# Loads of u and B reshaped from 36 rows three partitions apart to 64 rows two apart, with a staged part of zeros

## What is computed

```python
xc = silu(conv(normed @ in_proj_W) + conv_b)            # (8, 512, 256)
dt = clip(softplus(xc @ dt_W + dt_b), 0.001, 0.1)
Bp, Cp = xc @ B_W, xc @ C_W                             # (8, 512, 64)
def step(h, ins):                                       # 512 steps in sequence
    x_t, dt_t, B_t, C_t = ins
    h = exp(dt_t[..., None] * A) * h + dt_t[..., None] * B_t[:, None, :] * x_t[..., None]
    return h, einsum('ben,bn->be', h, C_t)
_, y = scan(step, h0, (xc, dt, Bp, Cp))
x = x + (y * silu(z)) @ out_proj_W ; x = x + feed_forward(x)
out = xn_input + block(xn) + binary_network(xn)
```

## Times and profile before

| | us |
|---|---|
| median of 3 runs | 1122.29 |
| lowest and highest run | 1107.89, 1122.53 |
| profiled execution, its own time | 1115.98 |
| its span, first to last instruction | 1114.2 |

### The profile page before, as it was taken

One profiled execution on the slowest core, in us unless ns is written; L12 is line 12 of the kernel. 1 busy time (PEld: TensorE's weight loads), 2 busy tenths in 40 slices (PEclk: granted clock), 3 DMA queues, 4 the chain that ended last, 5 costly groups with the idle time before them and its releaser, 6 DMA issues.

```text
span 1114.2 us, 27718 instructions
## 1 busy us (share of the span) xinstructions
PE 967.9 (87%) x8006; PEld 426.6 (38%) x8006; DVE 935.2 (84%) x2131; ACT 908.7 (82%) x1093; POOL 847.9 (76%) x1216
## 2 busy tenths in 40 slices
PE   5998883668999999998999887899998899999897
PEld 3555540113333343433333332334343334343436
DVE  5677663799989999997998887899998899999983
ACT  1666776789999999997988887899997899998980
POOL 6555513789888889887888786898887788988880
PEclk9999996789999999999999999899999899999999
DMA  4234358999999999997999999799999799999940
GB/s 139 81 136 180 136 200 298 345 327 355 351 343 334 345 355 350 345 344 268 356 341 332 319 328 318 271 351 352 353 349 333 280 366 343 339 356 340 335 148 10
DMA packets 76758, 327.39 MB, mean 294 GB/s; under 512 B 13472, under 2 KB 32800, under 8 KB 41504
## 3 DMA queue, kind: packets, MB, share of 16 engines
q1 hardware_dynamic: 76576, 325.30, 83.6%
HBM read 303.24 MB, written 22.02 MB: 292 GB/s over the span
## 4 chain that ended last, share of the span: by engine, by line
DVE 27%; PE 25%; POOL 19%; issue 16%; DMA 5%; ACT 5%; SPq 2%; DVEq 1%; POOLq 0%; ACTq 0%
POOL decayed L593 13%; DVE ps L1221 9%; PE ps L798 8%; DVE state L1232 7%; PE ps L743 5%; PE ps L897 5%; DMA decay<-dt_stage 4%; PE ps L883 3%; DVE h L1336 2%; ACT state L1030 2%; DVE h L1345 1%; DVE soft L1147 1%; POOL soft L543 1%; SPq L392 1%; POOL u_rest L553 1%
## 5 line engine op out<-in xcount | busy, mean ns | idle before, releaser
L593 POOL TENSOR_TENSOR decayed<-decay,state 128x256 f32<-128x256 f32 x1024 | 725.5, 733 | 169.1 <-DVE state L1232 125.4
L1010 ACT ACTIVATE decay<-decay,a_col 128x2048 f32<-128x2048 f32 x256 | 512.7, 2003 | 46.3 <-DMA decay<-dt_stage 36.5
L1232 DVE TENSOR_TENSOR state<-decayed,ps 128x256 f32<-128x256 f32 x1024 | 403.1, 417 | 55.4 <-POOL decayed L593 40.0
L1221 DVE TENSOR_TENSOR ps<-decay,ps 128x512 f32<-128x512 f32 x512 | 352.6, 689 | 40.5 <-ACT state L1030 17.2
L1030 ACT COPY state<-ps 128x512 f32<-128x512 f32 x512 | 288.9, 582 | 64.6 <-issue 43.2
L798 PE MATMUL ps<-state,c_cols 128*32 128x256 f32 x4096 | 338.2, 403 | 0.1
L743 PE MATMUL ps<-moving,b_rows 64*128 64x256 bf16 x1024 | 204.3, 281 | 100.5 <-DVE ps L1221 96.3
L750 PE MATMUL ps<-moving,b_rows 64*128 64x256 bf16 x1024 | 205.4, 282 | 12.0 <-DMA b_rows<-b_stage 12.0
L883 PE MATMUL ps<-h,w 128*128 128x256 f32 x512 | 175.8, 429 | 1.0 <-DVE h L1336 0.8
L743 PEld LDWEIGHTS ps<-moving,b_rows 64*128 64x128 bf16 x1024 | 58.4, 94 | 274.0 <-DVE ps L1221 172.3
L798 PEld LDWEIGHTS ps<-state,c_cols 128*32 128x32 f32 x4096 | 82.0, 109 | 113.4 <-issue 101.3
(11 more groups left out here) (124 smaller groups left out, 825.3 us busy)
## 6 DMA issues: line engine op xcount, KB each, us to landing
decay<-dt_stage SPq DMA_DIRECT2D x512, 512.0 KB, 6.6
moving<-u_stage SPq DMA_DIRECT2D x64, 288.0 KB
b_stage<-b_parts SPq DMA_DIRECT2D x24, 384.0 KB, 3.8
b_rows<-b_stage SPq DMA_DIRECT2D x64, 144.0 KB
dt_stage<-dt_tok SPq DMA_DIRECT2D x8, 512.0 KB, 3.1
u_stage<-u_parts SPq DMA_DIRECT2D x8, 512.0 KB, 2.8
x_tok<-in_L_attn_x_dram SPq DMA_DIRECT2D x4, 512.0 KB, 3.5
u_stage<-u_parts SPq DMA_DIRECT2D x8, 256.0 KB, 2.1
```

The costliest lines, as they stand in the source:

```text
L593: nc.gpsimd.tensor_tensor(decayed[:, p], decay[:, dec_slot(m, k), p, k % TS, :], state[:, (k - 1) % RING, p * E:(p + 1) * E], ALU.mult).th ...
L1010: nc.scalar.activation(pair, pair, ACT.Exp, scale=a_col[:, 2:3]).then_inc(decay_ready, 1)
L1221: nc.vector.tensor_tensor(ps[:, acc_bank(m, k), :].rearrange("p (q e) -> p q e", q=HQ), decay[:, dec_slot(m, k), HQ:Q, k % TS, :], ps[:, a ...
L1232: nc.vector.tensor_tensor(state[:, k % RING, p * E:(p + 1) * E], decayed[:, p], ps[:, SELFP + k % 2, p * E:(p + 1) * E], ALU.add).then_inc ...
```

## The change

`u_stage` and `b_stage` get a fourth part (NS = 4) along each dimension of parts, which holds zeros. It is written once, in the front, by 24 stores from a zeroed piece of `moving` (`store_pads`): for each of the 8 batches 256 KB to `u_stage`, and 512 KB and 384 KB to `b_stage`. `load_u` then moves 16 rows of 8 KB, each four times, and `load_b` 64 rows of 4 KB, both to the 64 partitions hq, hq + 2, hq + 4 and so on, which are the partitions of a dt transfer. All 128 rows of `moving` are now loaded, so that its two memsets go; a smaller one on POOL (2048 elements of a partition) makes the zeros for the stores.

```diff
-    ROWS = NP * NP * HALF
-    RSTEP = 3
-    RFIRST = HROW + RSTEP - 1 - RSTEP * (ROWS // 2)
+    NS = NP + 1
+    ROWS = NS * NS * HALF
+    assert HQ * ROWS == P
-    u_stage = nc.dram_tensor("u_stage", (HQ, HQ, 2, NP, T, E), BF16, kind="Internal").ap()
+    u_stage = nc.dram_tensor("u_stage", (HQ, HQ, 2, NS, T, E), BF16, kind="Internal").ap()
-    b_stage = nc.dram_tensor("b_stage", (HQ, HQ, 2, NP, NP, T, 2 * N), BF16, kind="Internal").ap()
+    b_stage = nc.dram_tensor("b_stage", (HQ, HQ, 2, NS, NS, T, 2 * N), BF16, kind="Internal").ap()
...
-            first = RFIRST - 2 + hq
-            return slice(first, first + RSTEP * (ROWS - 1) + 1, RSTEP)
+            return slice(hq, P, HQ)
...
-                         .unsqueeze(1).broadcast_to([HALF * NP, NP, TC * E])
+                         .unsqueeze(1).broadcast_to([HALF * NS, NS, TC * E])
...
+                def store_pads(n):
+                    q, bb = n // 2, n % 2
+                    u_rows, b_planes = u_stage[q % HQ, q // HQ, bb], b_stage[q % HQ, q // HQ, bb]
+                    zeros = moving[:, 1, 0:2 * NS].rearrange("p t e -> p (t e)")
+                    sp.dma_start(u_rows[NP].rearrange("(p j) e -> p (j e)", j=NJ),
+                                 zeros[:, 0:NJ * E]).then_inc(pads_stored, 16)
+                    sp.dma_start(b_planes[NP].rearrange("k (p j) n -> p k (j n)", j=NJ),
+                                 zeros[:, 0:NS * NJ * 2 * N].rearrange("p (k n) -> p k n", k=NS)).then_inc(pads_stored, 16)
+                    sp.dma_start(b_planes[0:NP, NP].rearrange("k (p j) n -> p k (j n)", j=NJ),
+                                 zeros[:, 0:NP * NJ * 2 * N].rearrange("p (k n) -> p k n", k=NP)).then_inc(pads_stored, 16)
...
+                sp.wait_ge(pad_zeroed, 1)
+                for n in range(B):
+                    store_pads(n)
...
                 sp.wait_ge(rows_zeroed, 2)
+                sp.wait_ge(pads_stored, 16 * PADS)
...
+                nc.gpsimd.memset(moving[:, 1, 0:2 * NS], 0.0).then_inc(pad_zeroed, 1)
...
-                    nc.gpsimd.memset(moving[:, 0], 0.0)
                     nc.gpsimd.memset(b_rows[:, 0], 0.0).then_inc(rows_zeroed, 1)
...
-                    nc.vector.memset(moving[:, 1], 0.0)
                     nc.vector.memset(b_rows[:, 1], 0.0).then_inc(rows_zeroed, 1)
```

More of the change, by code:

```diff
@@ L46, in mamba_and_binary_mlp_block @@
     HROW = P // 2
-    ROWS = NP * NP * HALF
-    RSTEP = 3
-    RFIRST = HROW + RSTEP - 1 - RSTEP * (ROWS // 2)
-    assert RFIRST > 0 and HROW + HQ - 1 + RSTEP * (ROWS // 2) <= P
+    NS = NP + 1
+    ROWS = NS * NS * HALF
+    assert HQ * ROWS == P
     QE = Q * E
@@ L118, in mamba_and_binary_mlp_block @@
         b_loaded = [sem("b_loaded0"), sem("b_loaded1")]
+        pad_zeroed = sem("pad_zeroed")
         rows_zeroed = sem("rows_zeroed")
+        pads_stored = sem("pads_stored")
         const_set = sem("const_set")
@@ L212, in mamba_and_binary_mlp_block @@
         STORES = 2 + NP
+        PADS = 3 * B
         def batches(eng, slot, filling=None):
```

## The result

| | median of the runs | profiled execution | its span |
|---|---|---|---|
| before | 1122.41 us | 1115.98 us | 1114.2 us |
| after | 1182.84 us (1179.76 to 1184.77) | 1184.77 us | 1183.0 us |

The account below looks back on a forecast made before the run. Engines were taken to set a floor of 27.05 us a chunk, with DMA binding now and then; 1116.0 - 17.3 + 2 - 1.5 - 1.5 gave 1097.7, say 1098 us. The forecast's own range was 1086 to 1106, the overall range 1086 to 1165.

Parts of the forecast that it names:

- The floor and the need: Scan: engines set 27.05 us a chunk (16 steps, 8 exps); after the change that needs 373 GB/s, up from 348.
- The sum: Whole kernel: 1116.0 us less 17.3, plus 2, less 1.5, less 1.5 gives 1097.7 us; chance 0.48.
- -1.5 for the front: Front: the `moving` memset on DVE goes, saving 1.5 us (0 to 2.1).
- +2 - 1.5 for the start: Scan's start: larger first u and B transfers cost 2 us; no longer slowing dt rows beside the second set saves 1.5.
- -17.3 for the rest: Scan outside the loop starts: stalls of the exps for dt go, saving 17.3 us (bounds 0 and 17.3).
- the 24 stores of zeros: Front: 11.8 us of SP's issuing and 9.4 MB of writes, covered by over 7 us, so costing 0.
- Bytes and marks: Chunk's transfers: 9.40 MB becomes 10.09 MB; u/B transfers go from 12 engines to 16, with 16 completion marks each.
- Why the mix is slow: Scan, u/B beside dt: rows clash by their SBUF partitions, not HBM addresses; rows with dt's footprint mix like dt.
- Rival A: Each chunk's u/B phase: the mix's rate stays low; 1144 us if loss is by transfer, 1254 by byte; chance 0.28.
- Evening out the engines: DMA engines, per chunk: 12 had 73 units of 8 KB and four had 64; after, all have 76.
- 15.3 us of loop starts: Three chunks beginning loop rounds take 15.3 us over three floors; DMA is not short there, so the change leaves them.
- rival B: Scan: in-between rate of 360 to 372 GB/s, chunks of 27.1 to 28.0 us, 1100 to 1126 us; chance 0.24.

Follow-up runs that it names:

- the run with one row: Kernel after, but every u and every B transfer reads one row broadcast to 64 partitions, products wrong: 1097.47 us, ratio 0.983.
- the run with 64 rows: Kernel after, but each u transfer reads 64 different adjacent rows in a two-dimensional pattern (64 x 4096), products wrong: 1099.65 us, ratio 0.982.
- the two versions with copies: Kernel before with u staged three times (36 x 4096): 1117.55 us; kernel after with u staged four times (64 x 4096): 1118.02 us.
- the run with rows seven apart: Kernel after with u in four transfers, seven of eight per chunk writing 16 rows seven partitions apart, products wrong: 1195.90 us, ratio 1.069.
- the four-transfer runs: Kernel after with each u transfer cut into four of 16 rows: eight partitions apart 1189.34 us, seven apart 1195.90, two apart 1212.67.

## Why the prediction was wrong

**The floor and the need: right.** 27.05 us a chunk and 373 GB/s are what the run with one row shows (54.20 us for two chunks at 375 GB/s).

**The sum: right in its total under its condition, in part by luck.** 1097.7 us was forecast; the four runs in which the mix is fast and nothing more is stored gave 1097.47, 1100.62, 1099.65 and 1099.19. In the profiled execution with 64 rows, 19.1 us shorter in span than that of before, the first exp starts 1.2 us earlier, the first chunk is 3.0 us shorter (33.2 for 36.2) and the rest of the scan 14.8 us; the sum had -1.5 for the front, +2 - 1.5 for the start and -17.3 for the rest, so two errors of about 3 us cancel. In the trace of after the first exp starts at 169.9 us, where it was 170.9, so the front gained 1.0 for the forecast 1.5, and the 24 stores of zeros cost nothing, as said. PE's longest wait for the first u is 13.7 us on the page of after, for 12.27: +1.4 for +2. SP issues a load of u in 0.6 us: the row count costs nothing.

**Bytes and marks: right.** 358.84 MB for 327.39 is 31.45 more; 32 chunks by 0.69 MB and 9.4 MB of zeros are 31.5. Small packets rise by 896 = 128 x 4 + 24 x 16: u and B transfers went from 12 engines to 16.

**"Why the mix is slow": the step that failed.** The prediction read 0.6 us at 362 GB/s as proof that u and B are not slow by themselves, concluded that they clash with dt rows through their partitions, and took it that rows with the footprint of dt mix like dt. On that step rests the term of -17.3 us. In its place the scan behind the first chunk became 67 us longer (937.2 for 869.8 us by the starts of the exps), and the exps' wait grew by 89 us. The footprint was given to u and B in the kernel after, and the plateau stayed (237 GB/s); the runs that changed only the source pattern removed it with the partitions untouched (424).

Nor does the kernel after need dt for it. SP issues the first four loads of u and B ahead of the chunk's dt, and by the count of its 8 KB packets no dt row starts before 180.9 us. First the kernel after, then the run with 64 rows, each from its first u packets to the end of this phase:

```profile
174.70:180.80 6.10, 0.00 (x0) 0.00 (x0) 0.00 (x0) 0.00 (x0) 0.78 (x2) 0.50 0.96 236
...
174.40:178.80 4.40, 0.00 (x0) 0.00 (x0) 0.00 (x0) 0.00 (x0) 0.88 (x2) 0.50 0.93 316
```

With u and B alone and the DMA engines 96 and 93% busy, the kernel after moves 236 GB/s, the other 316. So here the cause lies in the loads of u and B themselves and not in a clash with dt. In the kernel before it is otherwise: its first four loads have a median of 159 ns for a packet of 4 KB, as the run with 64 rows has, and its mix has 252. There the prediction's reading, that only the mix is slow, holds, although a stretch of 0.6 us was thin ground for it. What it could not give is the step from there to the new rows, whose load of u has 16 by 4 rows in place of 12 by 3. Rival A, with the plateau "at two places" and dt packets slowed on all engines alike, was the better evidence, and had a chance of 0.28. The third possibility, that the cost hangs on the form of one transfer's pattern, was not among the two that were considered ("where they lie in HBM", "where they go in SBUF"), although the diff carries it openly: u's load has an `unsqueeze` and a `broadcast_to`, B's is plain.

**Evening out the engines: not enough by itself.** The change did what it says: 16 engines instead of 12. In the kernel before that does count. With copies of u its form is two-dimensional and its mix is no faster, while the 32 by 2 form on 16 engines reaches 426 GB/s. So the layout of after is the better one, but only with a form that isn't 16 by 4: with plain rows in both, the scan has 337 GB/s in the layout of before and 364 in that of after (237.2 to 1054.3 us of the two versions with copies). Whether the 16 engines or the partitions two apart do this, no run tells, since both changed together; the prediction's idea of the partitions stays possible for this part.

**Rival A's price** was taken as loss by transfer (1144) or by byte (1254); 1183 lies between. From 237.2 to 1054.3 us there are 215 exps in place of 232. Less the 15.3 us of loop starts, that is 801.8 us for 26.9 chunks: 29.8 us a chunk. The prediction gave it a chance of 0.28 and set 365 GB/s as the rate of today's time; measured in that stretch are 333.

**The rules that were weighed.** The Trainium skill, "DMA: Bandwidth & Descriptors", "Latency and other measured facts", on power-of-two pitches: no effect at 256 and 128 KB, padded or not (1.053 and 1.002 against 1.058 and 1). So it was right to put it aside, though the slowness that it would have foretold came. The Trainium skill, "HBM Reference", "Specifications", gives about 358 GB/s as the share of a core when both cores of a pair stream, and about 425 for a core that streams alone; the prediction took only the first for its rival B. The traces agree with the second: 424 to 426 GB/s for 4 us with u, B and dt all under way, and 365 GB/s over 817 us in the fast versions. The Trainium skill, "SBUF — State Buffer", "Door 1: The DMA port swizzle", says that the rate depends on how many of 16 ports the partitions reach: the run with rows seven apart, which reach 14 by it in seven of eight transfers, didn't speed up over eight apart, which reach 8.

**Left open:** why 16 by 4 is slow and 32 by 2 is not; whether the four-transfer runs are slow by the same cause; and what keeps before's scan at 336 GB/s, 337 with two-dimensional loads of u: 12 engines, or partitions three apart.

## What to carry to other kernels

When several kinds of transfer share the DMA engines and the rate falls with all of them busy, change one transfer at a time to a single repeated row: two such runs found the culprit here. Compare the *forms* of the access patterns as well as bytes, partitions and addresses; here one load of 16 by 4 rows brought the rate from 424 to 241 GB/s in stretches of 4 us, and staging each row twice (32 by 2) was enough. Look for a stretch in which the suspected transfers run alone, and take a long one: 0.6 us was thin evidence on a rate, and copies that mend the load have a price at the place where they are stored.

## What was unexpected in the hardware

- The form of one load's source pattern changed the rate of what is in flight with it: 241 GB/s with u as 16 x 4 x 4096, 424 as 64 x 4096, 426 as 32 x 2 x 4096 in stretches of 4 us, with equal bytes, partitions and engines; 1184.95, 1099.65 and 1099.19 us. It needs no other traffic: u and B alone had 236 GB/s in the kernel after, 316 with u as 64 x 4096.
- 64 rows of 8 KB that lie 256 KB apart are read as fast as adjacent ones (landing 6.9 and 6.8 us).
- 36 rows three partitions apart, on 12 engines, slow the mix even as a plain pattern (252 GB/s in a stretch of 4.5 us), although their packets are fast while u and B are alone.
- Four transfers of 16 rows have 264 GB/s in the scan, no better than the one that they replace, and at the start, where SP takes 0.59 us to issue each 128 KB, the DMA engines are idle for 39%.
- Storing the zeros (8 x 1920 KB) batch by batch instead of at the head of the queue, with three stores of the last batch moved too, put the first exp off by 13 us (191.9 instead of 178.9).
